# Second layer of an audio tower: projection of q and k in quarters of the array from unrounded operands, k's heads exchanged, scores moved right behind it, and the FFN of the last two slots in other PSUM banks

## What is computed

```
q, k, v = x @ wq.T, x @ wk.T, x @ wv.T              # 16 heads of 64
proj    = einsum('bhnd,md->bhnm', x, omega)          # x is q or k; omega is 64 x 64
norm    = 0.5 * sum(x * x, axis=-1)
phi(x)  = exp(proj - norm) / sqrt(64)
out_n   = sum over m <= n of (phi_q[n] . phi_k[m]) v[m]  /  (sum over m <= n of phi_q[n] . phi_k[m] + 1e-6)
h       = h + out @ wo.T + bo
```

## Time and profile before

| | |
|---|---|
| median of 3 runs | 4551.7 us (4547.76 to 4551.86) |
| profiled execution: time | 4539.33 us |
| its span (first to last instruction) | 4536.7 us |
| its mean granted clock of TensorE | 0.983 |
| second layer in the span | from about 1646 us to the end |
| busy: PE, PEld, DVE, ACT, POOL | 96%, 88%, 73%, 60%, 46% |

### The profile page before, as it was taken

How to read it: one execution, slowest core, us unless ns; L and a number is a source line. 1 busy time by engine, 2 the same in 40 slices (tenths; PEclk the granted TensorE clock), 3 DMA queues, 4 the chain that set the end, 5 groups by cost and what they waited for, 6 DMA issues and landing times.

```text
span 4536.7 us, 121660 instructions
## 1 busy us (share of the span) xinstructions
PE 4354.9 (96%) x43948; PEld 3972.3 (88%) x43948; DVE 3317.8 (73%) x7106; ACT 2712.1 (60%) x5662; POOL 2100.0 (46%) x2682
## 2 busy tenths in 40 slices
PE   5999999999999958999999999999999999999997
PEld 4889999999899848899999999999999999989996
DVE  6999999999999845666666666666666666666665
ACT  4777777777777734555555555555555555545553
POOL 4566666666666522433433443343343344334333
PEclk8999999999999979999999999999999999999998
DMA  2100000000000010000000000000000000000000
GB/s 71 43 24 24 24 24 24 23 22 24 24 24 24 21 45 5 5 15 8 9 15 9 9 12 12 9 11 13 9 9 15 9 9 14 10 9 8 15 5 11
DMA packets 64982, 79.21 MB, mean 17 GB/s; under 512 B 8800, under 2 KB 51168, under 8 KB 64480
## 3 DMA queue, kind: packets, MB, share of 16 engines
q1 hardware_dynamic: 64608, 74.07, 5.6%
HBM read 49.40 MB, written 24.64 MB: 16 GB/s over the span
## 4 chain that ended last, share of the span: by engine, by line
PE 56%; DVE 3%; issue 2%; ACT 1%; POOL 1%; ACTq 0%; DVEq 0%; POOLq 0%
PE bA L1093 11%; PE bA L1095 9%; PE bA L1094 9%; PE bS L1398 4%; PE bO L1420 3%; PE bA L1484 3%; PE bB L1093 2%; PE bB L1094 2%; PE bB L1384 2%; PE bB L1095 2%; PE bB L1383 2%; PE bA L1485 2%; PE bT L1436 2%; PE bO L1424 1%; PE bO L1429 1%
## 5 line engine op out<-in xcount | busy, mean ns | idle before, releaser
L1820 POOL TENSOR_TENSOR sqs_lo<-sq,sqs_hi 128x768 fp32r<-128x768 f32 x256 | 480.6, 1878 | 673.9 <-ACT sqs_hi L1535 670.1
L1634 DVE TENSOR_TENSOR qk_lo<-bA,qk_hi 128x384 fp32r<-128x384 f32 x512 | 284.3, 556 | 517.1 <-ACT qk_hi L1535 516.8
L1554 ACT ACTIVATE phi<-bB 128x768 f32<-128x768 f32 x256 | 207.4, 810 | 662.5 <-PE bB L1384 662.5
L1778 POOL TENSOR_TENSOR yT_lo<-tanh_y,yT_hi 128x384 fp32r<-128x384 f32 x256 | 259.3, 1013 | 545.0 <-ACT yT_hi L1535 545.0
L1535 ACT ACTIVATE qk_hi<-bA 128x384 fp32r<-128x384 f32 x512 | 251.9, 492 | 195.2 <-PE bA L1095 188.0
L1644 DVE TENSOR_TENSOR aT<-bS,mask 128x1024 f32<-128x1024 f32 x256 | 311.0, 1215 | 1.3 <-PE bS L1403 1.3
L1544 ACT ACTIVATE sq<-bA 128x384 f32<-128x384 f32 x512 | 250.2, 489 | 62.1 <-DVE qk_lo L1634 61.3
L571 ACT ACTIVATE kblk<-gu,kb_masked,rowmask 128x128 f32<-128x128 f32 x752 | 271.7, 465 | 5.1 <-PE gu L452 5.0
L1093 PE MATMUL bA<-fc_lo,yT_hi 128*128 128x256 f32 x768 | 230.7, 300 | 13.1 <-POOL yT_lo L1778 6.4
L1093 PE MATMUL bA<-wv_lo,xT_hi 128*128 128x256 f32 x768 | 230.0, 300 | 5.9 <-ACT sq L1544 1.3
L1093 PE MATMUL bA<-wo_lo,attT_hi 128*128 128x256 f32 x768 | 226.3, 295 | 9.8 <-ACT sq L1544 2.1
(11 more groups left out here) (269 smaller groups left out, 16222.6 us busy)
## 6 DMA issues: line engine op xcount, KB each, us to landing
xT<-in_x SPq DMA_DIRECT2D x94, 256.0 KB, 2.6
h_scratch<-h SPq DMA_DIRECT2D x188, 64.0 KB, 1.9
hx<-h_scratch SPq DMA_DIRECT2D x32, 256.0 KB, 2.7
out<-res SPq DMA_DIRECT2D x32, 256.0 KB, 2.2
hx<-h_scratch SPq DMA_DIRECT2D x64, 64.0 KB, 2.4
out<-res SPq DMA_DIRECT2D x64, 60.0 KB, 1.8
q<-in_fc_q SPq DMA_DIRECT2D x2, 1024.0 KB, 7.7
wq_sb<-in_wq SPq DMA_DIRECT2D x1, 1024.0 KB, 5.0
```

The lines of the kernel that those rows point to most:

```text
L1634: dve.tensor_tensor(dst, src, hi.bitcast(fp32), ALU.subtract).then_inc(S[done], 1)
L1778: pool.tensor_tensor(yT[1][:, f % RING, :], tanh_y[f % 2][:], yT[0][:, f % RING, :].bitcast(fp32), ALU.subtract).then_inc(S["y_lo"], 1)
L1820: pool.tensor_tensor(sqs[1][:], sq[:], sqs[0][:].bitcast(fp32), ALU.subtract).then_inc(S["sq_lo"], 1)
```

## The change

- **Projection.** `omega2` is now 64 columns of omega on both halves of the partitions, and `norm2` is -0.5 everywhere, both fp32. `c2_proj` takes q and k and their squares as fp32, unrounded: 8 matmuls over 384 columns, each in a quarter. First four with omega, then four with norm2. For q (i = 0), the half r of the partitions goes to the output half r. For k (i = 1) it goes to the other half.
- **k's heads exchanged.** The two heads of a pair change places in `wk` on the host, so head h of k comes out of the projection on the same partitions as head h of q.
- **No splits.** `ec1` on ScalarE copies q and k (`qk_copied`) and `ec1b` squares both at once from SBUF (`sq_ready`). VectorE's `ec1`, the second square and the rounding on ScalarE, and the subtraction on GpSimd go. Place 0 waits for the copy in place of the square.
- **Scores** stand right behind the projection, ahead of `c1_qk`.
- **Last two slots' FFN.** In slots 30 and 31, `fc1` of odd f goes to B and `fc2` to SC. The lists of waits `read_b` and `read_s` belong to these.
- The preparation of omega and norm2 ahead of the loop falls away with its splits.

```diff
-        om, norm2 = split("omega2", [128, 128]), sb("norm2", [128, 128], fp32r)
+        om, norm2 = sb("omega2", [128, D1]), sb("norm2", [128, D1])
...
-        qk = split("qk", [128, 2, NT])
-        sq, sqs = sb("sq", [128, 2, NT]), split("sqs", [128, 2, NT])
+        qk, sq = sb("qk", [128, 2, NT]), sb("sq", [128, 2, NT])
...
+        def last_slots(s):
+            return isinstance(s, int) and s >= SLOTS - 2
+
+        def fc1_bank(s, f):
+            return B if last_slots(s) and f % 2 == 1 else A
+
+        def fc2_flat(s):
+            return SC_flat if last_slots(s) else A_flat
...
                 def c1_qk(s, c, g):
...
                         last.then_inc(S["qk_done"], 1)
-                        read[i].append(("qk_hi", 4 * g + (3 + i)))
+                        read[i].append(("qk_copied", 2 * g + (1 + i)))
 
                 def c2_proj(g):
 
-                    wait_g(pe, "sq_lo", g + 1)
+                    wait_g(pe, "sq_ready", g + 1)
                     wait_g(pe, "phi_ready", g)
-                    for i in range(2):
-                        o = B[:, i, 0:NT]
-                        product3(pe, o, [x[:] for x in om], [x[:, i, :] for x in qk], True, False)
-                        pe.matmul(o, norm2[:], sqs[1][:, i, :], start=False, stop=False)
-                        last = pe.matmul(o, norm2[:], sqs[0][:, i, :], start=False, stop=True)
+                    pe.sem_inc(S["proj_seen"], 1)
+                    for w, x, start in ((om, qk, True), (norm2, sq, False)):
+                        for i in range(2):
+                            for r in range(2):
+                                h = r if i == 0 else 1 - r
+                                last = pe.matmul(B[64 * h:64 * h + 64, i, 0:NT], w[64 * r:64 * r + 64, :],
+                                                 x[64 * r:64 * r + 64, i, :], start=start, stop=not start)
                     last.then_inc(S["proj_done"], 1)
...
+                    bank = fc1_bank(s, f)
+                    lists = read_b if bank is B else read
                     for k in range(KC):
-                        bank_free(k)
+                        bank_free(k, lists)
...
-                    rows_product(s, yT, fc2, j, "fc2_done", "out_ready")
+                    rows_product(s, yT, fc2, j, "fc2_done", "out_ready", fc2_flat(s), read_s if last_slots(s) else read)
...
                     if has_chunk(g - 1):
                         c2_proj(g - 1)
+                    if has_chunk(g - 2):
+                        c3_scores(g - 2, b)
                     if has_chunk(g):
                         c1_qk(s, c, g)
-                    if has_chunk(g - 2):
-                        c3_scores(g - 2, b)
                     run_place(table, s, c, 0, par)
...
             def _(act):
...
                 def ec1(g):
 
+                    wait_g(act, "proj_done", g)
                     for i in range(2):
                         act.wait_ge(S["qk_done"], 2 * g + (i + 1))
-                        copy(qk[0][:, i, :], A[:, i, 0:NT], "qk_hi")
-                    for i in range(2):
-                        act.wait_ge(S["qk_lo"], 2 * g + (i + 1))
-                        act.activation(sq[:, i, :], A[:, i, 0:NT], ACT.Square).then_inc(S["qk_hi"], 1)
+                        copy(qk[:, i, :], A[:, i, 0:NT], "qk_copied")
 
                 def ec1b(g):
-                    wait_g(act, "qk_hi", g + 1, 4)
-                    copy(sqs[0][:], sq[:], "sq_hi")
+                    wait_g(act, "qk_copied", g + 1, 2)
+                    act.activation(sq[:], qk[:], ACT.Square).then_inc(S["sq_ready"], 1)
...
             def _(dve):
...
-                def ec1(g):
-                    for i in range(2):
-                        dve.wait_ge(S["qk_hi"], 4 * g + (i + 1))
-                        low(qk[1][:, i, :], A[:, i, 0:NT], qk[0][:, i, :], "qk_lo")
-
...
             def _(pool):
...
-                    if has_chunk(g):
-                        wait_g(pool, "sq_hi", g + 1)
-                        pool.tensor_tensor(sqs[1][:], sq[:], sqs[0][:].bitcast(fp32), ALU.subtract).then_inc(S["sq_lo"], 1)
...
-        "omega": g["L1_attn_omega"].T, "wq": g["L1_attn_wq"].T, "wk": g["L1_attn_wk"].T, "wv": g["L1_attn_wv"].T,
+        "omega": g["L1_attn_omega"].T, "wq": g["L1_attn_wq"].T, "wk": g["L1_attn_wk"].reshape(CH, 2, D1, DM)[:, ::-1].reshape(INNER, DM).T, "wv": g["L1_attn_wv"].T,
```

More of the change, by code:

```diff
@@ L1168, in normalize @@
                                   ALU.subtract, ALU.mult).then_inc(S[name], 1)
[L1170 to L1191, removed]
-                    for i in range(2):
[L1193 to L1196, removed]
-                    for i in range(2):
[L1198 to L1201, removed]
-                    for i in range(2):
[L1203 to L1237, removed]
-                    dve.wait_ge(cstep, 1)
-                    for h in range(2):
-                        p = slice(64 * h, 64 * h + 64)
-                        dve.memset(half[p, p], -0.5).then_inc(cstep, 1)
-                    low(wq[1], w1["wq_sb"][:], wq[0], 1)
-                    low(wk[1], w1["wk_sb"][:], wk[0], 2)
-                    dve.wait_ge(S["h2_loaded"], 48)
-                    statistics(dve, 0, 0, hx, "stat3")
-                    low(wv[1], w1["wv_sb"][:], wv[0], 3)
-                    dve.wait_ge(S["rs3"], 2)
-                    normalize(dve, 0, 0, xn, hx, "xn_ready")
-                    low(wo[1], w1["wo_sb"][:], wo[0], 4)
-                    low(om[1], omega2[:], om[0], 6)
-                    dve.tensor_scalar(fc2b_bc[:], fc2b_bc[:], 0.5, None, ALU.mult).then_inc(cstep, 1)
@@ L1357, in _, with bank_free @@
             def _(pe):
-                read = [[], []]
-                def bank_free(i):
-                    for name, count in read[i]:
+                read, read_b, read_s = [[], []], [[], []], [[], []]
+                def bank_free(i, lists=None):
+                    for name, count in (lists or read)[i]:
                         pe.wait_ge(S[name], count)
-                    read[i].clear()
+                    (lists or read)[i].clear()
                 def c1_qk(s, c, g):
@@ L1480, in fc1, with rows_product @@
                         wait(pe, "hT_lo", s + 1, KC)
+                    bank = fc1_bank(s, f)
+                    lists = read_b if bank is B else read
                     for k in range(KC):
[L1482 removed]
+                        bank_free(k, lists)
                         w = fc1_w[:, k, 128 * f:128 * (f + 1)]
[L1484 to L1488 removed]
+                        pe.matmul(bank[:, k, 0:NT], w, hT[1][:, k, :], start=True, stop=False)
+                        pe.matmul(bank[:, k, 0:NT], w, hT[0][:, k, :], start=False, stop=True).then_inc(S["fc1_done"], 1)
+                        lists[k].append((f"pre_step{f % 2}", s * 8 + (2 * (f // 2) + (1 + k))))
+                def rows_product(s, lhs, w, j, done, added, flat=A_flat, lists=read):
                     for q in range(QT):
                         if q % 2 == 0:
[L1492 removed]
+                            bank_free(q // 2, lists)
                         for k in range(2):
[L1494 removed]
+                            last = product3(pe, tiles_flat(q, flat), [x[:, (2 * j + k) % RING, 128 * q:128 * (q + 1)] for x in lhs],
                                             [x[:, 2 * j + k, :] for x in w], k == 0, k == 1)
@@ L1696, in fc2_pair @@
                         wait(dve, "res_step", s + 1, 2)
[L1697 removed]
+                    add_rows(s, j, res[par], "fc2_done", "out_ready", fc2_flat(s))
                 def fc1(s, f):
```

90 lines of the change are left out of this document (70 added, 20 removed).

## The result

The changed kernel took 4350.18 us (median of 4 runs, 4347.73 to 4351.07), the one before 4550.93 us on the same chip (4 runs, 4547.76 to 4551.86). The ratio is 0.956, with a 95% interval of 0.954 to 0.958: 201 us less. The forecast was 4418 us, in a range from 4396 to 4480. The profiled execution took 4350.22 us, with a span of 4348.4 against 4536.7 before: 188.3 us less in the two traces that are compared here.

A forecast was written before the change was run, and what follows sets the result against it. TensorE, busy for 96% of the span, was taken as the bound. Savings of 100 + 10 + 3 + 13 + 8 = 134 us took the profiled 4539.3 to 4405 us, a median of 4418, range 4396 to 4480.

The forecast's parts named there:

- Term 1: Projection in each of 256 chunks: 1.74 us falls to 1.35 in quarters of the array, saving 100 us (79 to 118).
- Term 2: Passages into and out of quarters around projection and scores: `c4_av`'s way back to the whole array goes, 10 us (0 to 13).
- no gap between projection and scores: Sign on TensorE's timeline: scores follow the projection without a gap, and q's second matmul starts 0.28 us behind its first.
- The waits that change: TensorE's projection waits for the square, not GpSimd's remainder; the steady part has no such wait, 3 us gained (0 to 4).
- The 11.2 us for `xT_lo` stay: Steady part on TensorE: the wait for `xT_lo`, 11.2 us, was to remain unchanged.
- Term 3: First slots, before the FFN fills the places: mean projection wait falls from 2.1 to about 0.6 us, 13 us gained (8 to 20).
- Term 4: Last slots: `fc1` alternating between A and B gives 6 us, `fc2` not waiting for hT 2; together 8 us (0 to 14).
- Rival A: Projection: two row halves may not write one bank together, so eight rounds, 2.70 us; 4764 us in all, chance 9%.
- Rival B: Place 0, now directly behind k, waits for ScalarE's copy of q: 0.2 us a chunk lost, 4469 us, chance 22%.
- Rival C: Projection and scores together use no whole-array matmul, so the clock falls to 1.2 GHz for 3%: 4508 us, chance 5%.

## Why the prediction was wrong

**Term 1, the projection: right.** 1.35 us were worked out from the slopes of two other products, 1.34 came. Saved are 0.40 us a chunk (1.74 to 1.34), 102 us where the term had 100. (The table has 0.445, since its 1.785 holds the old waits and the way in from `c4_av` as well.) The run without the exchange shows that the rounds are what the term took them for.

**Term 2, in and out of the quarters: right in size, with one part left out.** The way in moved ahead of the projection and costs the FFN's last pitch +0.071 us a chunk. The way out moved to q and costs +0.016 with what k's end no longer pays. Place 0's first pitch is 0.10 shorter. The direct step from `c4_av` to the whole array is gone in two of eight steps. Of its 0.20 us only the 0.11 at the projection's first pitch came back, since `c4_av` still ends on a way into quarters, so 0.027. Together 0.040 us, 10 us as forecast. What the term did not have: directly behind other quarters the scores take 0.875 us, where they take 0.925 behind q and k. That is 0.05 us a chunk, 13 us. The sentence "no gap between projection and scores" was right, but no price was put on it.

**"The waits that change": this is the step that failed.** It spoke of the projection's wait and of `xT_lo`, and took the earlier trace rows for the whole of the waits. The wait of place 0 for the square was missing from the sum, since TensorE's own rows show 2.4 us of it: it was 0.12 us in every step, 30 us. The row of the loads names it 206 times, and the prediction shows no such row. It read the 1.03 us of the earlier trace rows as what the scores hold the array for. The kernel with the earlier square has 0.92 there, and was 34 us faster in all. In the other direction, "The 11.2 us for `xT_lo` stay" failed as well: 27.2 us. ScalarE's timeline after has, ahead of its copy for xT,

```profile
2775.38 0.52 ACT L1535 ACTIVATE yT_hi<-tanh_y 128x384 fp32r<-128x384 f32 x1 [0.72 <-DVE tanh_y L1702]
2775.81 0.85 ACT L1535 ACTIVATE xT_hi<-bA 128x384 fp32r<-128x384 f32 x2
```

and before

```profile
2782.65 0.53 ACT L1535 ACTIVATE yT_hi<-tanh_y 128x384 fp32r<-128x384 f32 x1 [0.16 <-DVE tanh_y L1709]
2783.08 0.85 ACT L1535 ACTIVATE xT_hi<-bA 128x384 fp32r<-128x384 f32 x2
```

The copy of y stands ahead and waits for VectorE's product, 0.72 us where it was 0.16. From the start of the transposes (2774.06 and 2781.90) to this copy it is 1.75 us and was 1.18: TensorE comes through the step sooner, and the FFN's chain on the other two does not; this is read from one step, and the run with fc1 moved forward shows only that the place of fc1 decides over the wait. In the table it is the +0.068 of `c4_av`, 17 us. `wo_pair`'s pitch gave another 7 us, unexplained.

**Term 3, the first slots: right in the waits, too small in all.** The waits of the projection fell from 18.7 to 3.6 us, about as forecast. But 29.9 us were won there. Most of the rest goes with the clock. Windows of 10 us of TensorE alone (busy, granted clock, DMA), before:

```profile
1680.00:1690.00 10.00, 5.55 (x22) 0.71 0.13 39
1690.00:1700.00 10.00, 9.25 (x64) 0.78 0.01 2
1700.00:1710.00 10.00, 7.38 (x78) 0.83 0.00 0
1710.00:1720.00 10.00, 8.27 (x61) 0.83 0.01 2
1720.00:1730.00 10.00, 8.62 (x122) 1.00 0.01 2
1730.00:1740.00 10.00, 8.20 (x59) 0.83 0.00 0
```

and after:

```profile
1680.00:1690.00 10.00, 8.74 (x106) 1.00 0.01 2
1690.00:1700.00 10.00, 9.54 (x121) 1.00 0.01 2
1700.00:1710.00 10.00, 9.86 (x157) 1.00 0.01 2
```

Before, five of the six windows have a mean between the clock's two levels (1.2 and 2.4 GHz), in a stretch in which TensorE stands idle again and again; after, the clock is 1.00 from 1680 us on, where TensorE is busy 8.7 to 10 of 10 us. At half the rate, a time t at a mean of 0.8 does work for 0.8 t: the missing shares of the six windows add up to 0.29 + 0.22 + 0.17 + 0.17 + 0.17 = 1.02, or 10 us at most, since a low clock costs nothing while TensorE is idle. Counted for its busy time alone, over the 24 chunks, the lower level took 11.0 us before and 1.5 after: 9.5 us. The time in which no matmul ran fell from 25.4 to 4.7 us there, 20.7, of which 15 are the projection's waits. Together that is 30 us, the 29.9 of the account. The forecast named the clock as what could push the term to its upper end of 20, and chose 13. No run took the clock apart from the waits, so its share is read from rows and not tested. The kernel with the scores behind q and k, which has the short chain too, has the same gain there (36.8 us in the first 24 chunks, of which 5.9 at its steady rate).

**Term 4, the last slots: right in size.** 8 us forecast, 8.6 in the trace, and 10 us (6 to 15 by the interval) with that edit alone. `fc1` gave 7.5 us where 6 were forecast; the 2 us for `fc2` did not show (31.2 us before, 32.2 after). The clock has a part in this stretch as well: its lower level took 9.6 us of busy time before and 7.9 after.

**The median.** The rows came from an execution of 4539.3 us, 12.4 faster than the median of its kernel, and the changed kernel's profiled execution lies on its median. So the medians differ by 201 us and the traces by 188: 12 to 13 of the 68 us of error lie outside the account of the terms. The run with the last slots alone has a trace on its own median (4541.08 and 4540.75 us), and it shows where the kernel before usually takes longer than in the trace that was read. The first matmul of q stands at 1672.6 us and not at 1669.3, the first 24 chunks take 249.4 us and not 246.3, and a chunk 10.936 and not 10.920: together about 10 us. To take 134 from the median was sound; 134 was read from an execution that had less to lose.

So the 134 us become the 188 between the traces as follows: the hidden wait +30, the round of the scores +13, the first slots +17, `wo_pair` +7, the growth of `xT_lo` -17, which leaves +4 in small ones; and 12 to 13 us more between the medians.

**The rivals.** Rival A, that two halves of the rows can't write one bank together, is refuted: 1.34 us and not 2.70 for the projection. The Trainium skill's TensorEngine Tiling (Array Packing), Gotcha 1: PSUM Pressure, lets no two row tiles access one bank at the same time; the trace does not agree for halves that write different partitions of the bank, and the time is not the 4764 us of rival A. The Trainium skill's PSUM — Partial Sum Buffer, PSUM bank collisions raise a hardware error, quotes the same strict rule, but reports a measured collision of row tiles only for one bank and the same quarter of the partitions; the trace agrees as far as it goes, with 1.34 us where the partitions differ. Nearly 2.7 us do come where only two quarters are in use, as the run without the exchange shows. Rival B, a new wait at place 0, did not come: no row has it, on PE or on the loads, and the first pitch there is 0.12 us. There it was the other way about, since the old wait was the one at that place. Rival C: the clock is 1.00 in the whole steady part.

## What to carry to other kernels

A wait shorter than a matmul's passage (0.12 us against 0.17 here), at a change between array shapes, was nearly absent from TensorE's row of waits: read the row of the weight loads beside it, and take the pitch of the last matmul ahead of each change of shape against the same change elsewhere. The row of the loads alone proves nothing. With the scores behind q and k it has

```profile
PEld bA L1093 <- DVE pre L1695: 34.7, 58, 0.6
```

where q follows the projection, and in these steps the projection takes 1.451 us to the start of q, exactly as in those in which the row names no releaser. Where an engine is full, work out a change from start-to-start times by kind of work, and count each entry into quarters (here 0.10 us) and each exit (here 0.11 us ahead of the next matmul, 0.10 behind it); keep products of one shape together. One profiled execution can lie 12 us from its kernel's median: a gain read from it is off by as much.

## What was not expected of the hardware

- An entry and an exit cost more than the 0.10 us each that the prediction read from the earlier trace rows: with the scores apart from the projection, 0.39 us a step, 100 us of 4350.
- The pitch of `wo_pair`'s 256-column matmuls has two values, 0.118 and 0.113 us, with the order of the products; `v_pair`, of the same shape, has 0.120 in both kernels.
- Both halves of the rows write into one bank, each at its own partitions, without loss: 1.34 us for the sixteen records.
- With only two quarters of the array at work a round is as long as with four, 0.335 us at 384 columns, and the next product's records start among the last of them (2802.64 and 2802.96 above).
- A hole that is closed in one place opened again at its neighbour: of the 27.2 us for `xT_lo`, one move of a place gave back 1 us, the other 20.
